# A four-layer graph network on one core: more dense chunks, 96-row ranges, narrower blocks, one-instruction tail one-hots, clears on ScalarE

## What is computed

```python
edge_index = jnp.stack([src, dst])          # dst sorted, dst = 12500 * u**2
# layer 0: sums over src of x[dst], weighted by a sigmoid of the head row and the edge type
x = _layernorm(x + tanh(segment_sum(att * x[dst], src) @ W0.T + b0))
# layers 1 to 3: sums over dst of x[src]
x = _layernorm(x + segment_sum(x[src], dst) @ W1.T + b1)
x = _layernorm(x + segment_sum(x[src] * edge_weight, dst))
x = _layernorm(x + segment_sum(x[src] * (edge_weight * edge_weight_n2), dst))
```

## Time and profile before

| | us |
|---|---|
| median of 3 runs (lowest, highest) | 12632.91 (12630.43, 12639.09) |
| the profiled execution, whole | 12637.55 |
| its span, first to last instruction | 12635.8 |
| scatter stretch of the first layer | 4314.1 |
| gather stretches of layers 1, 2, 3 | 2543.6, 2536.3, 2537.5 |
| busy: POOL, PE, DVE, PEld, ACT | 9429.6, 8760.5, 8319.3, 6387.1, 3617.1 |

### The profile page before, as it was taken

How to read it: one execution, slowest core, us unless ns; L and a number is a source line. 1 busy time by engine, 2 the same in 40 slices (tenths; PEclk the granted TensorE clock), 3 DMA queues, 4 the chain that set the end, 5 groups by cost and what they waited for, 6 DMA issues and landing times.

```text
span 12635.8 us, 165784 instructions
## 1 busy us (share of the span) xinstructions
PE 8760.5 (69%) x50360; PEld 6387.1 (51%) x50361; DVE 8319.3 (66%) x23044; ACT 3617.1 (29%) x8754; POOL 9429.6 (75%) x8321
## 2 busy tenths in 40 slices
PE   3766666666666625666666588888777688887776
PEld 2444545545545523445445555555555445555555
DVE  6766666666666557766665477776666677766665
ACT  2433232222222213222111045333222254332221
POOL 4888888888888817777777747777777577777775
PEclk6666666666656656676666679999988799999987
DMA  5333333333333331111111111111111111111111
GB/s 135 37 37 36 37 36 37 36 36 37 36 38 36 36 86 27 27 27 27 27 27 27 26 25 27 27 27 27 27 27 27 30 27 27 27 27 27 27 27 31
DMA packets 715298, 435.41 MB, mean 34 GB/s; under 512 B 514803, under 2 KB 612755, under 8 KB 713152
## 3 DMA queue, kind: packets, MB, share of 16 engines
q0 software_dynamic: 517920, 291.87, 19.2%
q1 hardware_dynamic: 195616, 132.68, 4.0%
q10 hardware_dynamic: 880, 0.23, 0.0%
HBM read 313.44 MB, written 110.74 MB: 34 GB/s over the span
## 4 chain that ended last, share of the span: by engine, by line
POOL 73%; issue 21%; PE 2%; DVE 2%; DMA 2%; SPq 0%; ACT 0%; POOLq 0%; DVEq 0%
POOL arena L626 45%; POOL table L570 27%; PE ps L946 1%; DMA table<-arena,idx 1%; PE ps L866 0%; DMA cmin_d<-cmin 0%; DVE arena L1258 0%; PE ps L965 0%; SPq L429 0%; PE ps L862 0%; DVE xs L1296 0%; DMA xt<-xs 0%; PE ps L958 0%; DVE arena L1263 0%; DVE stat L1282 0%
## 5 line engine op out<-in xcount | busy, mean ns | idle before, releaser
L626 POOL DMA_INDIRECT arena<-xt,src_i x6075 | 5766.5, 949 | 1909.6 <-issue 1850.6
L570 POOL DMA_INDIRECT table<-arena,idx x2225 | 3623.9, 1629 | 764.8 <-issue 669.7
L903 PE MATMUL ps<-arena 128*128 128x490 f32 (+1 forms) x5500 | 2576.5, 614 | 148.5 <-DVE arena L1376 106.7
L731 ACT ACTIVATE arena<-iota_f,src_i 128x128 f32<-128x128 f32 x3300 | 1036.5, 390 | 5167.8 <-PE ps L903 5167.0
L932 PE MATMUL ps<-arena 128*64 128x64 f32 (+1 forms) x12150 | 1150.5, 253 | 1898.4 <-DMA arena<-xt,src_i 1898.4
L932 PEld LDWEIGHTS ps<-arena 128*64 128x64 f32 (+1 forms) x12150 | 1006.3, 164 | 2520.5 <-DMA arena<-xt,src_i 2494.5
L1376 DVE TENSOR_SCALAR arena<-ps,dst_l 128x490 f32<-128x490 f32 (+1 forms) x3300 | 2248.7, 716 | 0.0
L916 PE MATMUL ps<-big,xs 128*64 128x64 f32 (+1 forms) x17052 | 2151.4, 304 | 12.3 <-DVE big L1388 12.3
L916 PEld LDWEIGHTS ps<-big,xs 128*64 128x64 f32 (+1 forms) x17052 | 2086.6, 167 | 14.8 <-DVE big L1388 14.8
L903 PEld LDWEIGHTS ps<-arena 128*128 128x128 f32 (+1 forms) x5500 | 990.4, 190 | 1184.6 <-issue 1128.6
L1394 DVE MEMSET big<- 128x1600 f32 (+1 forms) x348 | 475.0, 1365 | 1516.1 <-PE ps L916 1516.1
(11 more groups left out here) (159 smaller groups left out, 7439.2 us busy)
## 6 DMA issues: line engine op xcount, KB each, us to landing
arena<-xt,src_i POOLq DMA_INDIRECT x6075, 2.5
arena<-key_rows SPq DMA_DIRECT2D x445, 160.0 KB, 3.3
table<-arena,idx POOLq DMA_INDIRECT x2225
table<-arena POOLq DMA_DIRECT2D x3, 6304.0 KB
big<-table SPq DMA_DIRECT2D x42, 448.0 KB, 5.2
arena<-in_x_dram SPq DMA_DIRECT2D x445, 16.0 KB
xt<-xs SPq DMA_DIRECT2D x6, 1024.0 KB
arena<-in_x_dram SPq DMA_DIRECT2D x200, 1.2 KB
```

The lines of the kernel that those rows point to most:

```text
L570: pool.indirect_dma_start(out=tables[i % NTAB][:, :], out_offset=bass.IndirectOffsetOnAxis(ap=idx[:, i % (IDXS * GC):i % (IDXS * GC) + 1], ...
L626: pool.indirect_dma_start(out=gbuf[:, o:o + F], out_offset=None, in_=xt[l][:, :], in_offset=bass.IndirectOffsetOnAxis(ap=src_i[:, c:c + 1] ...
L731: ins = act.activation(lo_d[:, k * P:(k + 1) * P], iota_f[:, 0:P], ACT.Abs, bias=nslo[:, i * GC + k:i * GC + k + 1])
L903: last = pe.matmul(ps_d[b % PSD], lo_l[:, r * P:(r + 1) * P], blk_l[:, r * DT:(r + 1) * DT], start=(k == 0), stop=(k == parts - 1))
```

## The change

- `CD` goes from 1100 to 1300 and `C0` from 900 to 1000: 200 fewer gathers in each gather layer (1825, in 365 groups) and 100 fewer scatters (2125, in 425 groups).
- Blocks get 3, 4 or 5 destination rows by region and other sizes: 390 blocks of one chunk and 4 rows, 250 of one and 5, 200 of one and 3, 100 of two and 4, 40 of five and 4, 20 of three and 4: 1000 blocks in a gather layer, 700 in the first.
- Ranges of the gather layers are `WC` = 96 rows wide: 26 ranges. The first layer keeps 64-row ranges with lists of its own (24, before 20).
- A tail group's one-hots are one `tensor_tensor` of 128 x 320 from the iota in PSUM; weighted layers multiply by the weights in a second one, and `keys0` does the same.
- `dense` and `win` are cleared by ScalarE copies of a zero column, 128 x 96 x 25 for a zone and 128 x 20 x 128 in the first layer.
- Only one weight list lies in `big` at a time; the third layer's is loaded after the second layer's sums. Row values are read eight at a time from int16.

```diff
-CD = 1100
+CD = 1300
+WC = 96
-C0 = 900
+C0 = 1000
-PARTS = [(0, 300, (5,)), (300, 500, (3, 2)), (500, 755, (2, 2, 1)), (755, CD, (1, 1, 1, 1, 1))]
+PARTS = [(0, 200, (5,), 4), (200, 300, (3, 2), 4), (300, 500, (2, 2, 1), 4), (500, 700, (1, 1, 1, 1, 1), 3),
+         (700, 1050, (1, 1, 1, 1, 1), 4), (1050, CD, (1, 1, 1, 1, 1), D)]
...
-BLOCK_END, ZONE_END = slots(NBLK, [max(0.86 * k, 0.5 * k + 0.8) for _, k in BLOCKS], 25.0 / FZ, FZ, NT, 0)
+BLOCK_END, ZONE_END = slots(SEG_OF, [max(0.17 * k * d, 0.1 * k * d + 0.16 * d) for (_, k), d in zip(BLOCKS, ROWS_OF)],
+                            25.0 / FZ, FZ, NT, 0)
...
-        dense = y[:, 0:WD * T]
+        dense = big[:, 0:WC * T]
+        w_l = w12_c
...
-        ps_f = ps[:, 5 * BK:5 * BK + WD]
+        ps_f = ps[:, 5 * BK:5 * BK + WC]
...
+            def zone_clear0(z):
+                i = z % (NU // UZ) * UZ * 4
+                at = win_x[:, i:min(i + UZ * 4, T), :]
+                act.copy(at, zero_c[:, :].unsqueeze(2).to_broadcast([P, at.shape[1], P])).then_inc(cleared0, 1)
...
+            def clear(s_, l):
+
+                for z, (lo, hi) in enumerate(ZONES):
+                    act.wait_ge(flush_done[l], s_ * FZ + z + 1)
+                    act.copy(dense.rearrange("p (d s) -> p d s", s=T)[:, :, lo:hi],
+                             zero_c[:, :].unsqueeze(2).to_broadcast([P, WC, hi - lo])).then_inc(cleared[l], 1)
...
+                    while cleared_s < NSEG - 1 and i > -(-BLOCKS[SEGS[cleared_s + 1]][0] // GC):
+                        clear(cleared_s, l)
+                        cleared_s += 1
...
-                v.memset(win.rearrange("p (x s) -> p x s", s=T)[:, :, i:min(i + UZ * 4, T)], 0.0).then_inc(cleared0, 1)
...
-                    for k in range(GC):
-                        to = ohr[:, q + k * WD:q + (k + 1) * WD]
-                        if weight is None:
-                            ins = v.tensor_scalar(to, iota_f[:, 0:WD], dst_l[:, c + k:c + k + 1], None, ALU.is_equal)
-                        else:
-                            ins = v.tensor_scalar(to, iota_f[:, 0:WD], dst_l[:, c + k:c + k + 1],
-                                                  weight[:, c + k:c + k + 1], ALU.is_equal, ALU.mult)
-                    ins.then_inc(oh_done[l], 1)
+                    v.tensor_tensor(tail_oh(n), iota_p[:, 0:WD].unsqueeze(1).to_broadcast([P, GC, WD]),
+                                    bc(dst_l[:, c:c + GC], GC, WD),
+                                    ALU.is_equal).then_inc(oh_done[l] if weight is None else oh_plain[l - 1], 1)
+
+                def tail_weights(n, l=l, weight=weight):
...
+                    v.tensor_tensor(tail_oh(n), tail_oh(n), bc(weight[:, c:c + GC], GC, WD),
+                                    ALU.mult).then_inc(oh_done[l], 1)
...
-                    ins = v.tensor_scalar(blk_l[:, r * DT:(r + 1) * DT], iota_p, kd[:, c + k:c + k + 1], None,
+                    w = ROWS_OF[b] * T
+                    ins = v.tensor_scalar(blk_l[:, r * DT:r * DT + w], iota_p[:, 0:w], kd[:, c + k:c + k + 1], None,
...
-                    v.memset(dense.rearrange("p (d s) -> p d s", s=T)[:, :, lo:hi], 0.0).then_inc(cleared[l], 1)
```

More of the change, by code:

```diff
@@ L121, in gathered, with padded @@
     return (l * per_layer + n // R + 1) * 16 * GC
-ND = -(-NBLK // 4) * 4
-NTT = -(-NT // 4) * 4
+def padded(n):
+    return -(-n // 8) * 8
+ND, ND0, NTT = padded(NBLK), padded(NB0), padded(NT)
 NCB = CD - C0
-XB_AT = [min(n for n in range(NT0) if BLOCK0_END[n + 1] > SEGS[s_]) for s_ in range(NS0)]
+XB_AT = [min(n for n in range(NT0) if BLOCK0_END[n + 1] > SEGS0[s_]) for s_ in range(NS0)]
 def landed(n):
@@ L331, in program @@
                                                          ("oh_done", "agg_done", "acc_zero", "acc_add"))
+        oh_plain = [sem(f"oh_plain{l}") for l in range(1, 3)]
         lo_step = sem("lo_step")
@@ L352, in __init__ @@
                 self.eng, self.row, self.most = eng, row, most
-                self.r = [eng.alloc_register(f"{nm}{k}") for k in range(4)]
+                self.r = [eng.alloc_register(f"{nm}{k}") for k in range(8)]
             def value(self, i):
-                if i % 4 == 0:
-                    self.eng.load(self.r, self.row[:, i:i + 4])
-                return self.eng.snap(self.r[i % 4], min_val=0, max_val=self.most)
+                if i % 8 == 0:
+                    self.eng.load(self.r, self.row[:, i:i + 8])
+                return self.eng.snap(self.r[i % 8], min_val=0, max_val=self.most)
         class Fix:
@@ L675, in _ @@
                     act.wait_ge(m_done, n)
-                kw = D if G00 + n < G0 else WD
+                kw = rows_of((G00 + n) * GC)
                 act.copy(bts[0:kw, :], ps_bt[0:kw, :]).then_inc(bts_done, 1)
-                for u in range(ZONE0_END[n] * UZ, ZONE0_END[n + 1] * UZ):
-                    turned(u)
+                for z in range(ZONE0_END[n], ZONE0_END[n + 1]):
+                    for u in range(z * UZ, (z + 1) * UZ):
+                        turned(u)
+                    zone_clear0(z)
                 if n == 2:
@@ L746, in _ @@
                     ins.then_inc(lo_done[l], 1)
+                for s_ in range(cleared_s, NSEG):
+                    clear(s_, l)
                 for b in range(NB + 1):
@@ L790, in block_sums0 @@
                         q = (r * 2 + t) * P
-                        last = pe.matmul(ps_pair[b % 2][:, t * BK:t * BK + DT], lo0[:, q:q + P],
-                                         blk0[:, r * DT:(r + 1) * DT], start=(k == 0), stop=(k == parts - 1),
+                        last = pe.matmul(ps_pair[b % 2][:, t * BK:t * BK + w], lo0[:, q:q + P],
+                                         blk0[:, r * DT:r * DT + w], start=(k == 0), stop=(k == parts - 1),
                                          skip_group_check=True)
@@ L1013, in spread_row, with spread_bases @@
                     v.tensor_copy(cols, bc(row, m, k))
+            def spread_bases(row, to, bases, segs):
+                for s_ in range(len(segs) - 1):
+                    ins = v.tensor_copy(bases[:, s_:s_ + 1], row[:, segs[s_]:segs[s_] + 1])
+                link(ins)
+                link(v.tensor_scalar(bases, bases, float(N - (WC if segs is SEGS else WD)), None, ALU.min))
+                for s_ in range(len(segs) - 1):
+                    ins = v.tensor_copy(to[:, segs[s_]:segs[s_ + 1]],
+                                        bases[:, s_:s_ + 1].to_broadcast([1, segs[s_ + 1] - segs[s_]]))
+                link(ins)
             v.wait_ge(cmin_l, 16)
@@ L1019, in _ @@
             link(v.tensor_scalar(gmin, gmin, float(N - WD), None, ALU.min))
[L1020 to L1026 removed]
+            spread_bases(bmin, segb, sbase, SEGS)
@@ L1044, in _ @@
             link(v.memset(wlim[:, :], float(WD)))
-            v.memset(wlim[0:G0 // HQ, :], float(D))
+            for _, c1, _, rows in reversed(PARTS):
+                link(v.memset(wlim[0:c1 // CQ, :], float(rows)))
             v.memset(nb_i[:, :], 0)
@@ L1215, in _ @@
                 if n == G0 - G00 + 1:
-                    dense_keys(C0, CD, stat[:, 0:NCB].bitcast(I32))
+                    for lo in range(C0, CD, 2 * T):
+                        hi = min(lo + 2 * T, CD)
+                        dense_keys(lo, hi, stat[:, 0:hi - lo].bitcast(I32))
                 if n > 6:
```

198 lines of the change are left out of this document (109 added, 89 removed).

## The result

The changed kernel takes 12404.06 us (median of 4 runs, 12401.48 to 12406.52), the kernel before 12631.67 us beside it: a ratio of 0.9819, 95% interval 0.9802 to 0.9836. It is faster, as forecast, but by 228 us and not by 878: 649 us over the predicted time and 464 above the range.

What follows compares the result with a forecast made beforehand. Indirect DMAs on POOL were taken to set the time, with the dense side becoming the bound in weighted layers. Terms -193 - 155 + 15 + 8 - 245 - 308 = -878 us gave 11755 us, range 11540 to 11940.

Steps and rivals of the forecast that it cites:

- The first layer: Scatter stretch: 100 fewer scatters -193 us, clears off DVE -155, ScalarE's clears +15, set-up rows +8, together -325.
- my +15: First layer: cost of two ScalarE clears in a row with their flush, +15 us, bounds 0 and 120.
- The flush: Weighted gather layer, PE: flush matmuls of 96 columns cost 0.18 us each, bounds 0.123 and 0.185; 917 us a layer.
- One-hots 701 "less 26 x 10 x 0.54, 561": Weighted gather layer, DVE: 701 us of one-hots, ten per range made during the flush, leaving 561.
- The sum: Dense side of a weighted gather layer: 2342 us, 2382 with two additions of 20; unweighted layer 2298.
- The slow clock: Weighted gather layer: slow clock in a sixth of the stretch, where a dense chunk takes PE longer than DVE, +20 us.
- ScalarE late at every range: Gather layers: ScalarE's clears delay its low one-hots by one group, 3.9 us in 78 ranges, +300 us: 12055; chance 0.17 with other longer chains.
- my sign for this rival: Gather layers: a range's first add coming over 4 us after the last flush matmul would show late ScalarE.
- the other rivals: Flush matmul not dearer, 11555 us, chance 0.20; destinations outside narrowed blocks running end loops, 1.5 ms a group, 0.02.
- The range: Whole kernel: 11540 to 11940 us, taking in the cheap flush and half of the late ScalarE.

Runs made afterwards that it cites:

- flush_adjacent: late_rows4 with the flush matmuls reading 96 columns side by side instead of 98 elements apart, clears writing them so too: 11531.88 us (0.9142).
- late_rows4: The changed kernel with next-range one-hots made after the range's last add and gather-layer row values read four at a time from int32: 11803.99 us (0.9349).

## Why the prediction was wrong, step by step

- **The first layer: right.** 2125 scatters with mean 1553 ns, none held back by clears: -338 us against -333. The clear on ScalarE takes 5.03 us, my upper bound and not the 2.34 or 2.2 of the copies; the scatters waited 93 us for ScalarE's message copies in place of 74.5, so +18 for my +15. With its start, a copy to single elements 98 apart takes 1.97 ns an element here.
- **The flush: right.** 0.187 us against 0.18. It is the term that I called decisive; from the last add of a range to the next range's first add 40.3 us pass above (8009.27 to 8049.56), 40.9 on the mean, by my terms (917 + 76 + 62) / 26 = 40.6. What I read of the column's price was right, and flush_adjacent shows that it is the price of columns that lie apart. One row was read too simply: in the flush at 8164.54 the granted clock fell to 0.65; the next, at 8171.30, ran at 1.00 and took 6.31 us, so the conclusion stands. The Trainium skill (SBUF — State Buffer, Door 1: The DMA port swizzle) has a penalty for accesses that each fall in another 16-byte line. The trace agrees, with 0.10 us for 96 columns; but no run varied the distance, so that the line is the cause isn't shown.
- **One-hots 701 "less 26 x 10 x 0.54, 561": wrong, the first failed step.** I read "at most ten ahead" as ten made during the flush. The list makes a one-hot behind each add, so the ring is full when the flush begins, and DVE idles in it. It did so before the change too; DVE's one-hots (L1376) in the flush of the earlier trace rows, 8164.54 to 8190.50, count, ns, first and last start:

```profile
L1376 DVE TENSOR_SCALAR arena<-ps,dst_l x2: 715/716/718, 8164.4 to 8165.0; 128x490 f32<-128x490 f32 x2
```

  That is two, where I counted ten, and my sum for the kernel before had the same fault. With all 1300 one-hots between the flushes the term is 701. The repair brought 76 to 80 us in each weighted layer and not 140, as an add that directly follows another waits for it and takes 0.22 us longer, a price that my sum didn't have either.
- **Row loads: missing, the second failed step.** The change's list names them ("read eight at a time from int16"), my sum has no term, though the order and the lines stood there. 136 us in each weighted layer, 100 in the other. It was an operation in a new form and should have had bounds: from below nothing, as one of 0.34 us hides beside an add, and from above some multiple of it times 175 a layer, all of it on DVE's list between the flushes.
- **The sum.** Weighted: 2382 predicted, 2624.4 measured; 136 are the loads, 80 the order, the other 26 are left and no run explains them. Unweighted: 2298 and 2471.9; 100 and 72, 2 left. The paces themselves held where adds and one-hots alternate (add 0.47, one-hot 0.54, a tail group 1.05 for 1.03).
- **The slow clock** (+20): the granted clock is 0.96 in the weighted layers where I had taken 0.92, and 1.00 in late_rows4. So there was less slow clock than I put in; no run prices what was left of it.
- **Rival "ScalarE late at every range": wrong as a mechanism.** The first add came 2.4 us after the last flush matmul (8047.11 to 8049.56), as in the sum, and 3.1 on the mean of a weighted layer's ranges, +18 us in each. Five of 25 took over 4 us, my sign for this rival; but with int32 loads none does (3.3 at most), so it was a load in the handover. Its size, +300, lay nearest to the truth by chance. No edge fell outside a window, and the flush matmul did get dearer, so the other rivals fell too.
- **The range** was built from the unknown prices that I had noticed. Both misses are in what I had taken as known: the time between the flushes of a weighted layer is 480 + 561 + 246 + 20 = 1307 us by my terms and 1547 in the trace, 18% more, and had no bounds of its own.

## What to carry to other kernels

When a change takes away the slack of one side, everything on the other side that was free must be priced anew: also queue work such as register loads, and also idle time whose length was never looked at. Where a list is "n ahead", look in the trace at whether the work ahead is done in the gap, since a ring that is filled in step with the consumer is already full when the gap comes. In a diff, each operation whose operand type or count changes needs a term of its own, however small the line. And where work is taken out from between two dependent instructions, price the wait that it covered.

## What the runs showed of the hardware

- A register load on DVE's queue: 0.342 us for four int32 values, 0.596 for eight, 0.946 for four int16, 1.827 for eight. Int16 values cost 0.22 us each, int32 values 0.06. The loads run beside the add and one-hot of 1.0 us: 0.6 us is hidden, 0.95 not fully.
- A float32 matmul with 96 columns that lie 98 elements apart: 0.186 us (50 in 9.31), side by side 0.084, both at a granted clock of 1.00.
- A memset on DVE held back indirect scatters with addition (mean 1629 against 1553 ns over all, 2585 for those beside one) but not the indirect gathers of the later layers (946 ns beside one, 953 for the others).
- A DVE add that waits for the add before it starts 0.13 us after its end: 0.80 us from start to start at 490 columns, 0.69 at 392, where with a one-hot between the two the add costs 0.58 and 0.47.
- DVE's memset and ScalarE's copy to runs of 25 elements take about the same, 2.06 and 2.25 us for 128 x 2400; ScalarE to single elements 98 apart 5.03 us for 2560.
